# A routed two-layer network on one core: the first batch's weights of y made first, a two-tensor form for the root's correction, idle products in two early gaps, and another order of x's blocks and maxima

## The reference

```python
def cond(Efou, y, weight):                      # Efou = x (2, 1024, 256), y = cond (2, 256)
    ys = y * (1.0 / np.sqrt(np.float32(weight.shape[0])))
    d = jax.lax.rsqrt(jnp.einsum('bi,io->bo', ys * ys, weight * weight) + 1e-8)
    return jnp.einsum('bsi,io->bso', Efou * ys[:, None, :], weight) * d[:, None, :]

def ffn(x, router_w, router_b, lang_w, lang_b, w1, b1, w2, b2):
    lang_probs = jax.nn.softmax(x @ lang_w.T + lang_b, axis=-1)
    lp_pad = jnp.pad(lang_probs, ((0, 0), (0, 0), (0, 1)))
    idx = jnp.arange(8) % 4
    router_logits = x @ router_w.T + router_b + 0.1 * (lp_pad[..., idx] + lp_pad[..., idx + 1])
    top_p, top_i = jax.lax.top_k(jax.nn.softmax(router_logits, axis=-1), 2)
    top_p = top_p / top_p.sum(axis=-1, keepdims=True)
    h = jax.nn.gelu(jnp.einsum('bsd,edh->bseh', x, w1) + b1, approximate=False)
    expert_out = jnp.einsum('bseh,ehd->bsed', h, w2) + b2
    sel = jnp.take_along_axis(expert_out, top_i[..., None], axis=2)
    return (top_p[..., None] * sel).sum(axis=2)

out = x + ffn(cond(x, cond_1024, L0_cond_weight), ...)
```

## Time and profile before

| | |
|---|---|
| median of 3 runs | 295.92 us (294.46 to 297.45) |
| profiled execution | 298.01 us |
| its span, first to last instruction | 296.3 us |
| mean granted clock of TensorE | 0.964 of full |
| TensorE busy | 272.3 us (92%) |
| VectorE, ScalarE, POOL busy | 190.8, 194.8, 177.6 us |

### The profile page before, as it was taken

One profiled execution on the slowest core, in us unless ns is written; L12 is line 12 of the kernel. 1 busy time (PEld: TensorE's weight loads), 2 busy tenths in 40 slices (PEclk: granted clock), 3 DMA queues, 4 the chain that ended last, 5 costly groups with the idle time before them and its releaser, 6 DMA issues.

```text
span 296.3 us, 8970 instructions
## 1 busy us (share of the span) xinstructions
PE 272.3 (92%) x3066; PEld 222.3 (75%) x3066; DVE 190.8 (64%) x427; ACT 194.8 (66%) x426; POOL 177.6 (60%) x161
## 2 busy tenths in 40 slices
PE   8899988889999999999999999999999989999810
PEld 6777877588889899788877777877777767777500
DVE  2846688979999898565555555655655655655610
ACT  3246449599897898767667677567577667677600
POOL 8200037780678888877877778767767757445230
PEclk9579999999999999999999999999999999999975
DMA  6999994559894443645453553743544433422230
GB/s 159 375 391 357 326 350 120 178 199 451 314 296 83 61 84 75 94 75 88 74 83 66 73 93 57 77 86 57 87 79 73 74 74 59 66 42 22 36 35 0
DMA packets 39497, 39.93 MB, mean 135 GB/s; under 512 B 19504, under 2 KB 35328, under 8 KB 39296
## 3 DMA queue, kind: packets, MB, share of 16 engines
q1 hardware_dynamic: 31872, 28.89, 32.5%
q0 software_dynamic: 7552, 10.45, 22.1%
q10 hardware_dynamic: 32, 0.01, 0.0%
HBM read 27.61 MB, written 9.64 MB: 126 GB/s over the span
## 4 chain that ended last, share of the span: by engine, by line
PE 84%; DVE 4%; DMA 3%; POOL 2%; issue 2%; ACT 1%; DVEq 0%; POOLq 0%
PE ps L643 34%; PE ps L660 31%; PE ps L539 6%; PE ps L652 4%; PE ps L557 4%; DMA rows<-y_rows,idx 1%; DMA out<-onehot,idx 1%; POOL rows L439 1%; PE ps L481 1%; PE ps L512 1%; PE ps L620 1%; DVE wsp L951 1%; PE ps L521 1%; DVE dv L882 1%; ACT wsp L781 1%
## 5 line engine op out<-in xcount | busy, mean ns | idle before, releaser
L643 PEld LDWEIGHTS ps<-onehot,wsp 128*128 (+1 forms) x1872 | 129.3, 98 | 36.7 <-issue 3.3
L643 PE MATMUL ps<-onehot,wsp 128*128 128x128 f16 x1872 | 153.1, 219 | 2.2 <-issue 1.5
L827 ACT ACTIVATE pay<-ps,cur 128x128 f32<-128x128 f32 x312 | 117.2, 462 | 51.8 <-issue 37.9
L660 PE MATMUL ps<-wsp,pay 128*128 (+1 forms) x616 | 138.0, 316 | 1.2 <-DVE pay L1113 1.2
L470 POOL DMA_INDIRECT out<-onehot,idx x39 | 73.5, 1883 | 27.0 <-POOL onehot L461 10.6
L1113 DVE SCALAR_TENSOR_TENSOR pay<-pay,cur 128x512 f16<-128x512 f32 x72 | 54.5, 758 | 29.4 <-ACT pay L815 28.1
L439 POOL DMA_INDIRECT rows<-y_rows,idx x39 | 51.4, 1317 | 20.1 <-issue 11.3
L461 POOL TENSOR_SCALAR onehot<-onehot,cur 128x256 f32<-128x256 f32 x36 | 36.3, 1009 | 27.6 <-DVE onehot L1131 26.7
L660 PEld LDWEIGHTS ps<-wsp,pay 128*128 128x128 f16 x616 | 46.2, 98 | 6.1 <-issue 1.7
L1107 DVE TENSOR_SCALAR pay<-pay,cur 128x512 f16<-128x512 f32 x36 | 19.3, 535 | 25.3 <-ACT pay L827 25.3
L1126 DVE SCALAR_TENSOR_TENSOR onehot<-ps,cur,b2bc 128x256 f32<-128x256 f32 x36 | 17.4, 483 | 15.1 <-PE ps L660 11.7
(11 more groups left out here) (176 smaller groups left out, 201.4 us busy)
## 6 DMA issues: line engine op xcount, KB each, us to landing
stage<-in_L_ffn_w SPq DMA_DIRECT2D x9, 1024.0 KB, 10.6
wsp<-in_L_ffn_w SPq DMA_DIRECT2D x7, 1024.0 KB, 11.2
y_rows<-pay SPq DMA_DIRECT2D x4, 512.0 KB, 7.8
wsp<-in_x SPq DMA_DIRECT2D x3, 512.0 KB, 7.9
b2bc<-in_L_ffn_b SPq DMA_DIRECT2D x1, 1024.0 KB, 5.2
rows<-y_rows,idx POOLq DMA_INDIRECT x39, 3.1
out<-onehot,idx POOLq DMA_INDIRECT x39, 4.1
wsp<-in_x SPq DMA_DIRECT2D x2, 256.0 KB, 5.6
```

What stands on the lines that cost most here:

```text
L643: last = mm(ps[:, HB + (2 * j + g) % RING, c * P:(c + 1) * P], wsp[:, bass.ds(e, 1), o:o + P].rearrange("p a f -> p (a f)"), xsp[:, j % RI ...
L660: last = mm(ps[:, OB + j % 2, 0:width], hsp[:, (2 * j + g) % NH, part, c, :], wsp[:, bass.ds(e, 1), o + w:o + w + width].rearrange("p a f ...
L827: last = a.activation(to, ps[:, HB + (2 * j + g) % RING, c * P:(c + 1) * P], ACT.Gelu, bias=cur[:, j % CURS, cc:cc + 1], scale=cur[:, j % ...
```

## The change

- `halves3`, a tile with 1.5 in it, is set by POOL, and L882 becomes a scalar_tensor_tensor that reads it, in place of a tensor_scalar with two constants.
- Eight idle products are put ahead of `transpose_x(0)` and four ahead of `transpose_x(1)`.
- The rows of d and the weights of y are made batch by batch: TensorE does d's rows of batch 0 (bank 3), the router's columns, then d's rows of batch 1 (bank 5). VectorE makes the weights of batch 0 first, then takes two maxima of x, then makes the weights of batch 1. `wyr_ready` counts to 2; y's tiles 0 to 3 wait for 1.
- `transpose_x(2)` follows the rows of d, and one `transpose_x` follows each of y's tiles 0 to 4. ScalarE's copies all come before the scaled copies; its preload of the exponential's table stands after the third.
- The transpose of b1 and the scale's two small products follow `transpose_x(7)`. VectorE copies b1 and takes its maximum after the scale.

```diff
@@ POOL
             g.memset(ones[:, :], 1.0).then_inc(ones_ready, 1)
+            g.memset(halves3[:, :], 1.5).then_inc(warm_ready, 1)
@@ TensorE
+            keep_warm(8, 5, 256)
             transpose_x(0)
+            keep_warm(4, 5, 256)
             transpose_x(1)
+
+            def rows_of_d(b):
+                for o in range(KD):
+                    last = mm(ps[:, (3, SB)[b], o * P:(o + 1) * P],
+                              dcol[:, o, b:b + 1].broadcast_to([P, P]), ident[:, :], start=True, stop=True)
+                last.then_inc(d_psum, 1)
+
             pe.wait_ge(d_ready, 1)
-            for b in range(NB):
-                for o in range(KD):
-                    last = mm(ps[:, 3, b * D + o * P:b * D + (o + 1) * P],
-                              dcol[:, o, b:b + 1].broadcast_to([P, P]), ident[:, :], start=True, stop=True)
-            last.then_inc(d_psum, 1)
-            transpose_x(2)
+            rows_of_d(0)
             pe.wait_ge(rd_ready, 1)
...
             last.then_inc(wr_psum, 1)
-            transpose_x(3)
+            rows_of_d(1)
+            transpose_x(2)
...
-            pe.wait_ge(wyr_ready, 1)
             for t in range(T):
+                pe.wait_ge(wyr_ready, 1 if t < LB else 2)
                 rows_of_y(t)
-                if t == 1:
+                if t in (0, 1, 2, 3):
+                    transpose_x(3 + t)
+                if t == 4:
+                    transpose_x(7)
                     pe.wait_ge(b1_in, 16)
                     tr(ps[:, SB, BM:BM + E * KF], b1r[:, :], ident[0:E * KF, 0:E * KF]).then_inc(b1_psum, 1)
-                    transpose_x(4)
-                if t == 3:
-                    transpose_x(5)
                     pe.wait_ge(ym_ready, 1)
                     tr(ps[0:1, SB, YMAX:YMAX + P], ysm[:, :], ident[:, :]).then_inc(ym_psum, 1)
-                if t == 4:
                     pe.wait_ge(y_max, 1)
                     mm(ps[:, SB, YS:YS + 1], ones32[0:1, :], ymax[0:1, 1:2], start=True, stop=True).then_inc(ys_psum, 1)
-                    transpose_x(6)
-                    transpose_x(7)
+                if t == 5:
                     pe.wait_ge(b1_ready, 1)
@@ VectorE
-            step(v.tensor_scalar(dv[:, 3, :], dv[:, 4, :], -0.5, 1.5, ALU.mult, ALU.add))
+            dve.wait_ge(warm_ready, 2)
+            step(v.scalar_tensor_tensor(out=dv[:, 3, :], in0=dv[:, 4, :], scalar=-0.5, in1=halves3[:, :], op0=ALU.mult, op1=ALU.add))
...
+            weights_of_y(0)
+            max_of_x(0)
+            max_of_x(1)
+            weights_of_y(1)
             for c in range(2, len(XCHUNKS) - 1):
                 max_of_x(c)
```

More of the change, by code:

```diff
@@ L152, in adaln_moe @@
         dcol = sb("dcol", [P, KD, NB])
+        halves3 = sb("halves3", [P, KD * NB])
         b1r = rows[0:E * KF, 2, 0:P]
@@ L741, in copy_xt @@
                              ACT.Copy).then_inc(xt_ready, 1)
-            for q in range(4):
+            for q in range(T // 2):
                 copy_xt(q)
-            a.activation(warm[:, :], dv[:, 0, 0:1], ACT.Exp)
-            copy_xt(4)
-            copy_xt(5)
+                if q == 2:
+                    a.activation(warm[:, :], dv[:, 0, 0:1], ACT.Exp)
             def gram_sums(g):
@@ L787, in _ @@
                 a.activation(y_halves[:, t, 0, :], ps[:, t % BANKS_Y, 0:D], ACT.Copy, scale=yscale[:, 0:1]).then_inc(y_high, 1)
-                if t in (2, 4):
-                    copy_xt(5 + t // 2)
             act.wait_ge(lang_in, 1)
@@ L896, in max_of_x, with weights_of_y @@
                                 apply_absolute_value=True).then_inc(x_max, 1)
-            for c in range(2):
-                max_of_x(c)
-            dve.wait_ge(d_psum, 1)
-            for b in range(NB):
+            def weights_of_y(b):
+                dve.wait_ge(d_psum, b + 1)
                 for k in range(KD):
                     v.scalar_tensor_tensor(out=Wyr[:, b, k, 0:D], in0=W[:, k, :], scalar=ys[:, k, b:b + 1],
-                                           in1=ps[:, 3, b * D:(b + 1) * D], op0=ALU.mult, op1=ALU.mult)
-            dve.wait_ge(wr_psum, 1)
-            wr = ps[:, LB, 0:KD * NB * NR].rearrange("p (k b n) -> p b k n", k=KD, b=NB)
-            for b in range(NB):
-                last = v.tensor_tensor(Wyr[:, b, :, D:], wr[:, b, :, :], ys[:, :, b:b + 1].broadcast_to([P, KD, NR]), ALU.mult)
-            last.then_inc(wyr_ready, 1)
+                                           in1=ps[:, (3, SB)[b], 0:D], op0=ALU.mult, op1=ALU.mult)
+                dve.wait_ge(wr_psum, 1)
+                wr = ps[:, LB, 0:KD * NB * NR].rearrange("p (k b n) -> p b k n", k=KD, b=NB)
+                v.tensor_tensor(Wyr[:, b, :, D:], wr[:, b, :, :], ys[:, :, b:b + 1].broadcast_to([P, KD, NR]),
+                                ALU.mult).then_inc(wyr_ready, 1)
+            weights_of_y(0)
+            max_of_x(0)
+            max_of_x(1)
+            weights_of_y(1)
             for c in range(2, len(XCHUNKS) - 1):
                 max_of_x(c)
-            dve.wait_ge(b1_psum, 1)
-            step(v.tensor_copy(tab[:, :, 0:KF], ps[:, SB, BM:BM + E * KF].rearrange("p (e c) -> p e c", e=E)))
             dve.wait_ge(x_max, len(XCHUNKS) - 1)
             v.tensor_reduce(ysm[:, :], xmax[:, :], AX.X, ALU.max).then_inc(ym_ready, 1)
-            v.tensor_reduce(bmx[:, :], tab[:, :, 0:KF], AX.X, ALU.max, apply_absolute_value=True).then_inc(b1_ready, 1)
             dve.wait_ge(ym_psum, 1)
@@ L927, in _ @@
                             ALU.add).then_inc(ys_ready, 1)
+            dve.wait_ge(b1_psum, 1)
+            step(v.tensor_copy(tab[:, :, 0:KF], ps[:, SB, BM:BM + E * KF].rearrange("p (e c) -> p e c", e=E)))
+            v.tensor_reduce(bmx[:, :], tab[:, :, 0:KF], AX.X, ALU.max, apply_absolute_value=True).then_inc(b1_ready, 1)
             v.tensor_scalar(yg[:, 0:1], yt[:, :], -float(FIELD_GELU), None, ALU.add)
```

## The result

| | before | changed |
|---|---|---|
| median of 6 runs | 295.77 us (294.46 to 297.45) | 299.06 us (297.05 to 300.44) |
| ratio, 95% interval | 1 | 1.0085 [1.0044, 1.0126] |
| profiled execution, its span | 298.01, 296.3 us | 300.06, 298.3 us |
| mean granted clock | 0.964 | 0.970 |

The change made the kernel slower, by 0.4 to 1.3%, where 295.3 us was forecast; 299.06 lies above the range as well.

The account below looks back on a forecast made before the run. TensorE was taken to bound the loop, so only an earlier start could gain: 0.13 + 2.13 - 1.17 + 0.25 = 1.34 us, halved to 0.65 off the 295.92 median, giving 295.3 us, range 293.5 to 297.6.

Parts of the forecast that it names:

- From then on both kernels have the same eleven tiles to do: From the scaled copies on, y's last eleven tiles, bound by TensorE, take the same time in both kernels (24.72 to 35.40).
- nothing, or 0.1 at most: Cost in us of b1's copy and maximum on VectorE behind the scale, two operations of some 0.2 each.
- The root's correction: L882 on VectorE takes 0.17 us instead of 1.90 despite POOL's iota; the 1.73 saved is hardly on the path.
- The idle products: Twelve products ahead of x's first pairs cost 0.6 us on the path (eight take 0.95) and hold the upper clock.
- Rival B: The idle products don't hold TensorE's clock at 8.8 us; scaled copies 2.8 later, 298.7 us; chance 1 in 10.
- The order up to the scaled copies: y's tiles alternate with transposes from 12.28, ysm's transpose at 20.4, scaled copies at 22.05, 1.3 us earlier than before.
- rival A: TensorE's clock falls in the wait for y's scale; 1.1 to 2.2 us lost, 295.7 to 296.8 us; chance 3 in 10.
- The wait is shorter than the thin work before the fall: Argument against a clock fall at y's scale: 3.3 us of waiting against thin TensorE work from 4.35 to 8.7.
- The sum, halved for the median: A gain of 1.34 us on the profiled execution, taken as 0.65 for the median, giving 295.3 us.
- C: Typical runs of before already keep the upper clock; the change is then 1.9 us slower, 297.8; chance 2 in 10.
- 2.13 by the clock: Gain in us from d's rows to y's first tile (3.04 against 5.17), by the clock and a later transpose.
- A microsecond won before y's last eleven tiles moves the end by a microsecond: Time won ahead of those tiles reaches the kernel's end in full, unless something else is late by then.

Follow-up runs that it names:

- e5: The kernel before with only the root's two-tensor form; median 295.68 us, ratio 0.9971 [0.9925, 1.0016] to the kernel before.
- r1: The kernel before run again, unchanged, for a second trace; median 295.35 us, ratio 0.9991 [0.9951, 1.0031] to the kernel before.
- r2: The changed kernel run again, unchanged; median 299.56 us, ratio 1.0121 [1.0066, 1.0176] to the kernel before.
- e7: The changed kernel without its twelve idle products; median 298.36 us, ratio 1.0028 [0.9983, 1.0074] to the kernel before.
- e1: The changed kernel with VectorE's reduction of b1's maxima behind y's tile 3 instead of tile 0; median 297.04 us, ratio 1.002 to the kernel before.
- e3: The changed kernel with idle products in the wait for y's scale and b1's reduction behind tile 3; median 296.97 us, ratio 1.0027 to the kernel before.
- e4: The kernel before with only the root's two-tensor form and the twelve idle products; median 294.91 us, ratio 0.9985 [0.9949, 1.0021] to the kernel before.
- e2: The changed kernel with 3 and 12 idle products around the scale's small product; median 297.06 us, ratio 1.0007 [0.9959, 1.0054] to the kernel before.
- e9: e4 with the last weight's gram behind the loop's first block, and more idle products behind the routing; median 298.21 us, ratio 1.0057 to the kernel before.
- e10: The kernel before with the last weight's gram behind the loop's first block, and more idle products; median 299.00 us, ratio 1.0077 to the kernel before.
- e8: e4 with four idle products ahead of the routing tables' wait and five instead of ten behind the last gram; median 296.01 us, ratio 0.9979.

## Why the prediction was wrong, step by step

The step that failed first is "From then on both kernels have the same eleven tiles to do", together with "nothing, or 0.1 at most" for b1's copy and maximum: the eleven tiles took 4.04 us more. That alone turns a gain of 1.34 into a loss. The second is the start that the gain was counted from.

**The root's correction: right.** 0.16 us inside the iota (forecast 0.17). The rule of the Trainium skill, "SBUF — State Buffer", section "Who interferes with whom", is borne out: the form with two SBUF inputs isn't held up by an iota that only writes. In the changed kernel it gave nothing on the path, as forecast, since the rows of d started at 10.95; in e5, without idle products, they started at 8.79 (9.38 in r1).

**The idle products: wrong in size where the clock came late.** Eight cost 1.89, not 0.95, and the transposes 1.06, since the clock wasn't up at 7 in this trace; I had concluded from 0.66 at 6.50 that it always would be. In r2 it was up, and they took 1.06 and 0.60. Hence y's first tile at 13.17 and not 12.28 (11.87 in r2). Rival B's deciding point, 2.4 GHz at 9.5, was missed by the durations of the first trace, four idle products at 9.56 still taking 1.06; but the clock came at about 10.5 and not at 19, and held to y's scale, so B's price fell away. That these products are what holds it isn't shown: e7 and r1 had it without them.

**The order up to the scaled copies: right by luck, as two errors cancelled.** 21.80 (22.05 forecast), though y began 0.9 late: from there to ysm's transpose it took 7.0 us, not 8.1. I had charged 0.94 and 0.62 per tile and transpose, 1.56 together; in the trace a pair of tile and transpose comes every 1.34 (13.17, 14.52, 15.86).

**b1's copy and maximum, "nothing, or 0.1 at most": wrong, 1.1 us.** I priced their own durations (0.21 and 0.22) and not the transpose of their result, L594, which the change moves behind tile 5 while VectorE's reduction keeps its place behind tile 0. The rows of the order ahead show L594 there; the text never asked who waits for it, nor what stands behind that on VectorE.

**"From then on both kernels have the same eleven tiles to do": wrong, 4.04 us.** This is rival A with the wait on top. A's place was exact (tile 5 at about 23.4; it was 23.13, and the clock fell at 24.2). Its price was too low: half of 4.5 us at most, from the one rise seen before, where the lower level lasted 6.8 us in the changed kernel, 6.8 in r2 (21.2 to 28.0) and 3.4 in e1 and e7. And 3 in 10 was too low a chance: all four profiles without products in this wait fell (changed, r2, e1, e7), neither of the two with them did, nor any of the eight profiles with the order of before, where tile 4 and transposes fill the wait. "The wait is shorter than the thin work before the fall" was no reason against it. The Trainium skill, "TensorE: Matmul & The Clock Gate", section "HAM oscillation — how this bites in real kernels", tells of a clock that is lost in the waits between bursts of products, and spoke against the change. The falls at 24.2 here and at 21.2 in r2, in and behind such a wait, agree in kind.

**The sum, halved for the median: the wrong start to count from.** The two profiled executions alone have the sign already (a loss of 2.0 us in place of 1.34 won). The further 1.3 of the medians comes from here. A and C were taken for cases of which one holds, but they add. In r1 C's condition held in the main: the scaled copies of this run of before, near its median, came at 20.12, where C had worked out 20.2. That it is so close is luck in part, as the rows of d took 1.79 there and not 1.30. C's price of 1.9 was too high, because the changed kernel's copies come at 20.50 in r2 and not at 22.05; the order costs 0.4 there, and up to 1 at y's end (e3 against e4). Then comes A, with b1's wait, 3.8. The forecast compared with the lower level of 8.8 to 19 of one trace that was 2.2 us above the median, and the gain it credited, 2.13 by the clock, was for the most part not there to win.

**"A microsecond won before y's last eleven tiles moves the end by a microsecond": right for later, wrong for earlier.** 2.45 later gave 2.0. Of what came earlier, e4's 5.0 us gave 2.6 at the first rows, and e3's gain over r1 none: the weight's load lands at 49.2 or later, as SyncE's queue comes to the last two loads no earlier than 35.4, and the earlier trace rows, read from a late start, couldn't show a load that was not yet late.

**What stays open.** Why TensorE's clock comes up at 4 or 5 in some executions and 10 or 12 in others, of the same instructions; why the low stretch lasted 6.8 us in two profiles and 3.4 in two; why e1, e2 and e3 share one median although their profiles' y's ends lie 4.4 us apart, which the load's floor and the rank of the profiled executions account for in part only; and e7's spread. Whether the clock's rise alone makes the 3 us over which the runs of before lie isn't shown either. But in the twelve profiles other than e9's and e10's it took 238.5 to 239.8 us from the first transposed rows to the end, so what told these executions apart lay ahead of the loop.

## What to carry to other kernels

Where an edit moves one half of a pair (TensorE's transpose behind tile 5) and leaves its reader in place (VectorE's reduction behind tile 0), follow both programs until they meet again, and price the wait, not the durations. Work that seems to be in the way of a short dependent chain may be what keeps TensorE's clock up: take it out only if something else stands there, as the fifteen idle products of e2 did. Before a gain is summed against one trace, see whether that execution is a typical one; here the second trace of the same kernel was 3 us shorter, and most of the gain that was forecast had already been in it.

## What the runs showed of the hardware

- The same program had its granted clock at 0.50 from 8.8 to 19.0 in one execution; in another (r1) its durations are those of 2.4 GHz from about 11 on. The scaled copies lie 3.3 us apart.
- The clock column can read 1.00 where the durations are of 1.2 GHz, up to the first change that it shows: in r1 eight records of d took 1.79 at 9.38, in e4 1.06, both under a column of 1.00.
- TensorE with three small products in some 3 us (busy 0.45, 0.38 and 0.00 in the windows from 20 to 23) went to 1.2 GHz at 24.2, 1.1 us after its next tile had started, and stayed there for 6.8 us, the most of it full work, at 1.9 us for a tile instead of 0.94. In e1 and e7 it stayed 3.4 us. In e2, with fifteen idle products in this stretch, it stayed at 2.4 GHz.
- A load of 1 MB (median 11.6 us from issue to landing in e4) landed at 49.2 to 51.0 in the five profiles whose chain goes through it (y's end from 30.4 to 33.0), and not in step with y's end: at 50.38 for 30.72 (e8) and 50.35 for 32.13 (r1). Once y ends by 32 the start of the loop hardly follows it.
